# Local attention with 64-row transposes and four heads turned together, and the engine orders of that stage written anew

## The reference, cut to what matters

```python
# B, N, DIM = 8, 256, 128 here; DEPTH = 2, HEADS = 8, DIM_HEAD = 64, WINDOW = 64
h = shift_token(x)
q, k, v = split(h @ wqkv)                     # 8 heads of 64
q, k = l2norm(q) * qs, l2norm(k) * ksc
q, k = rotary_xpos(q, k)
# each window of 64 queries sees its own 64 keys and the 64 before
sim = einsum('bhwid,bhwjd->bhwij', bq * 8, bk)
mask = (i < j) | (i > j + WINDOW) | (j == -1)
attn = softmax(where(mask, -big, sim))
o = einsum('bhwij,bhwjd->bhwid', attn, bv)
x = x + o @ wo
h = layernorm(shift_token(x)) * lg + lb
a, g = split(h @ w1 + b1)
x = x + (a * gelu(g)) @ w2 + b2
```

## Time and profile before

| | |
|---|---|
| median of 3 runs | 911.72 us (910.61 to 911.75) |
| the profiled execution, its own time | 911.55 us |
| its span, first to last instruction | 909.8 us (so 1.7 us lie around it) |
| instructions | 22,535 |
| PE / PEld busy | 766.4 (84%) / 560.2 us (62%) |
| DVE busy | 662.8 us (73%) |
| ACT busy | 589.8 us (65%) |
| POOL busy | 527.3 us (58%) |
| mean granted TensorE clock | 0.930 of full speed |
| local attention stage (first to last `scores1`) | from 499.6 to 878 us |
| in it, one step | 23.9 us |

### The profile page before, as it was taken

The page is one execution under the profiler, slowest core; times in us unless marked ns, Lnnn a source line. Parts: engine busy times, 40 slices in busy tenths (PEclk is TensorE's granted clock), DMA queues, the critical chain, the costliest instruction groups (busy, mean ns, idle before and its releaser), DMA issues. The chain is left out here.

```text
span 909.8 us, 22535 instructions
## 1 busy us (share of the span) xinstructions
PE 766.4 (84%) x7262; PEld 560.2 (62%) x7262; DVE 662.8 (73%) x1986; ACT 589.8 (65%) x1784; POOL 527.3 (58%) x603
## 2 busy tenths in 40 slices
PE   5999999999987629946655789999999999998884
PEld 3666766666677528835532456666666666665564
DVE  5788888888858665535754677887888888877555
ACT  3688888888811107733433678888888888877660
POOL 4644545555435853348717677777777777776411
PEclk9999999999999759975877899999999999999998
DMA  8455444444300753421100000000000000000001
GB/s 216 159 181 180 161 173 169 168 175 163 127 2 16 236 165 91 115 65 44 32 1 0 1 1 2 2 2 1 1 2 1 2 2 1 2 1 2 13 2 35
DMA packets 61855, 61.71 MB, mean 68 GB/s; under 512 B 13243, under 2 KB 50606, under 8 KB 61614
## 3 DMA queue, kind: packets, MB, share of 16 engines
q1 hardware_dynamic: 59694, 56.10, 18.7%
q0 software_dynamic: 2048, 4.20, 1.5%
HBM read 17.55 MB, written 23.00 MB: 45 GB/s over the span
## 5 line engine op out<-in xcount | busy, mean ns | idle before, releaser
L641 POOL TENSOR_TENSOR scratch<-scratch 128x256 f32<-128x256 f32 (+1 forms) x128 | 105.7, 826 | 110.7 <-DVE scratch L1627 110.7
L1018 ACT ACTIVATE scratch<-psum,scratch 128x128 f32<-128x128 f32 x256 | 113.8, 458 | 49.4 <-DVE scratch L1974 47.6
L769 POOL TENSOR_TENSOR big<-big 128x512 f32<-128x512 f32 x64 | 81.2, 1269 | 70.6 <-DVE big L1955 70.6
L873 ACT ACTIVATE scratch<-psum,scratch 128x256 f32<-128x256 f32 x256 | 117.5, 479 | 3.6 <-DVE scratch L1645 3.6
L778 POOL TENSOR_TENSOR scratch<-scratch,mhalf 128x16 f32<-128x16 f32 x32 | 92.9, 2905 | 16.5 <-DVE scratch L1961 16.5
L1946 DVE TENSOR_REDUCE scratch<-big 128x8 f32<-128x512 f32 x64 | 43.7, 683 | 46.6 <-ACT big L992 46.6
L1125 PE MATMUL psum<-scratch 128*64 128x256 f32 x480 | 62.1, 379 | 1.6 <-DMA scratch<-xT 1.6
L1638 DVE TENSOR_TENSOR psum<-psum,causal 128x512 f32<-128x512 f32 x64 | 44.8, 699 | 20.4 <-PE psum L1149 20.1
L1149 PE MATMUL psum<-scratch 64*128 64x128 f32 (+1 forms) x512 | 59.2, 350 | 0.0
L1175 PE MATMUL psum<-scratch 128*64 128x256 f32 (+1 forms) x512 | 55.7, 338 | 2.2 <-DVE scratch L1633 2.2
L992 ACT ACTIVATE big<-psum 128x512 f32<-128x512 f32 x64 | 38.5, 602 | 29.0 <-PE psum L1398 28.1
(11 more groups left out here) (288 smaller groups left out, 2212.3 us busy)
## 6 DMA issues: line engine op xcount, KB each, us to landing
routed_in<-zfill SPq DMA_DIRECT2D x64, 256.0 KB, 2.3
scratch<-w_qkv SPq DMA_DIRECT2D x60, 193.0 KB, 2.2
scratch<-xT SPq DMA_DIRECT2D x60, 128.0 KB, 2.1
scratch<-routed_in SPq DMA_DIRECT2D x47, 64.0 KB, 1.8
routed_out<-scratch SPq DMA_DIRECT2D x23, 128.0 KB, 1.9
big<-in_L_ffn_W SPq DMA_DIRECT2D x1, 2048.0 KB, 8.7
stream<-in_L_attn_resid_pre SPq DMA_DIRECT2D x4, 256.0 KB, 3.9
big<-in_L_ffn_b SPq DMA_DIRECT2D x1, 1024.0 KB, 12.2
```

The lines of the kernel that those rows point to most:

```text
L641: pool.tensor_tensor(y, y, rs[s][:, t, :].unsqueeze(2).to_broadcast([P, 2, n]), ALU.mult).then_inc(b_p, 1)
L769: pool.tensor_tensor(qk[s][t][:, j * INNER:(j + 1) * INNER], t1[i % 2], t2[i % 2], ALU.add).then_inc(f_add, 1)
L873: last = act.activation(pr[s][:, t, h, :], scores_of(s)[:, h, t * S:(t + 1) * S], ACT.Exp, bias=nb[s][:, 2 * t + h:2 * t + h + 1], accum_o ...
L1018: last = act.activation(p1[k][:, h, t, :], bank(h)[:, t * P:(t + 1) * P], ACT.Exp, bias=nb1[k][:, h, t:t + 1], scale=rq8[s][:, t, 2 * a + ...
```

## The change

Four things are done together.

1. **q/k transposes.** `turn_qk` now has two pieces a unit (`half_` = 0, 1), each of which turns q and k of two pairs (four heads) with 16 transposes of 64 rows: rows 0 to 63 into bank 5, rows 64 to 127 into bank 3. ACT copies each bank out (`turned_out`, two copies of 512 columns a piece). It now waits for the rotated q too, and for DVE to have emptied bank 3.
2. **Probability transposes.** `turn_probs1` also has two pieces, each turning two pairs with 16 transposes of 64 rows into banks 2 and 3. It waits for both pairs' normalisation. ACT copies bank 2 (`probs_out`), DVE bank 3; `values1` does two pairs (12 products) at once into bank 2 and waits for both copies; `z_out` copies two pairs at once. `p1` has four buffers in place of two, `pt1` one that holds two pairs.
3. **The mask.** `scores1` writes the mask with four 64-row, 64-column products for a pair in place of two 128-row ones; the second array half needs the mask with its two row halves exchanged, `band_swapped`, which two DMAs from `band` fill near the start.
4. **The orders** of PE, ACT and DVE in a step are written anew; POOL's is the same.

```diff
             sp_.wait_ge(const_ready, 2)
+            load(band_swapped[0:WIN], band[WIN:P])
+            load(band_swapped[WIN:P], band[0:WIN])
...
             def expo(m, s, a):
                 act.wait_ge(f_nb, m * 4 + a + 1)
-                if later(m * 4 + a - 1):
-                    act.wait_ge(f_t, m * 4 + a - 1)
+                if later(m * 2 + a // 2 - 1):
+                    act.wait_ge(f_t, m * 2 + a // 2 - 1)
...
-            def probs_out(m, a):
-                act.wait_ge(f_t, m * 4 + a + 1)
-                act.activation(pt1[0].rearrange("p h t n -> p (h t n)"), bank(2), ACT.Copy).then_inc(f_pt0, 1)
+            def probs_out(m, half_):
+                act.wait_ge(f_t, m * 2 + half_ + 1)
+                act.activation(turned_probs_half(0), turned_probs(0), ACT.Copy).then_inc(f_pt0, 1)
...
+            def turn_qk(m, s, half_):
+                if half_ == 0:
+                    pe.wait_ge(f_kn, m + 1)
+                    pe.wait_ge(f_add, m * 4 + 4)
+                    pe.wait_ge(f_v, m * 2 + 2)
+                elif live(m + 2):
+                    pe.wait_ge(f_hT, m + 3)
+                if later(m * 2 + half_ - 1):
+                    pe.wait_ge(f_pt1, m * 2 + half_ - 1)
+                for j in range(2):
+                    for b_ in range(2):
+                        for t in range(TB):
+                            for r in range(2):
+                                rows = slice(r * DH, (r + 1) * DH)
+                                o = (j * PAIRS1 + 2 * half_ + b_) * P
+                                c = (j * 2 + b_) * P + t * DH
+                                mm = pe.transpose(bank(QK_TURNED[r])[:, c:c + DH], qk[s][t][rows, o:o + P], ident[rows, rows])
...
-                for h in range(2):
-                    pe.matmul(bank(h)[:, 0:S], identb[:], band[:].rearrange("p t n -> p (t n)"), start=True, stop=False,
-                              skip_group_check=True)
+                for u in range(2):
+                    for h in range(2):
+                        rows = slice(h * DH, (h + 1) * DH)
+                        pe.matmul(bank(h)[u * WIN:(u + 1) * WIN, 0:S], identb[rows, rows],
+                                  (band if u == h else band_swapped)[rows].rearrange("p t n -> p (t n)"),
+                                  start=True, stop=False, skip_group_check=True)
...
+            def turn_probs1(m, half_):
+                pe.wait_ge(f_p, m * 2 + half_ + 1)
+                pe.wait_ge(f_pp, m * 2 + half_ + 1)
+                if later(m * 2 + half_):
+                    pe.wait_ge(f_zsb, m * 2 + half_)
+                if half_ == 0:
+                    pe.wait_ge(f_trs, m * 4 + 4)
+                elif live(m + 1):
+                    pe.wait_ge(f_trs, m * 4 + 6)
+                for a in range(2):
+                    for h in range(2):
+                        for t in range(TB):
+                            for r in range(2):
+                                rows = slice(r * DH, (r + 1) * DH)
+                                mm = pe.transpose(turned_probs(r)[:, (a * 2 + h) * TB + t, :],
+                                                  p1[2 * half_ + a][rows, h, t, :], ident[rows, rows])
...
+            def values1(m, s, half_):
+                pe.wait_ge(f_pt0, m * 2 + half_ + 1)
+                pe.wait_ge(f_pt1, m * 2 + half_ + 1)
...
+                for a in range(2):
+                    for v, t, o, n in ((v1[s][:, 0, :], 0, 0, P), (vmid[s], 1, 0, WIN), (v1[s][:, 1, :], 1, WIN, WIN)):
...
+            def turned_out(m, s, half_):
...
+                for u in range(2):
+                    act.activation(qkT1[s][:, :, 2 * half_:2 * half_ + 2, u * P:(u + 1) * P],
+                                   bank(QK_TURNED[u]).rearrange("p (j b n) -> p j b n", j=2, b=2), ACT.Copy).then_inc(f_trs, 1)
...
+        def turned_probs(r):
+            return bank(2 + r).rearrange("p (b n) -> p b n", n=DH)
+        def turned_probs_half(r):
+            return pt1.rearrange("p a h t n -> p (a h t) n")[:, :, r * DH:(r + 1) * DH]
+        QK_TURNED = (5, 3)
...
             def step(n, s):
+                if live(n - 1): z_out(n - 1, 1 - s, 1)
                 if live(n + 2): square(n + 2, 0)
-                if live(n - 1): z_out(n - 1, 1 - s, 3)
-                if live(n): turned_out(n, s, 3)
                 if live(n): expo(n, s, 1)
+                if live(n + 1): value_out(n + 1, 1 - s, 0)
+                if live(n + 1): value_out(n + 1, 1 - s, 1)
                 if live(n): probs_out(n, 0)
...
                 if live(n - 1): gelus(n - 1)
+                if live(n): probs_out(n, 1)
                 if live(n + 2): square(n + 2, 3)
                 if live(n + 1): expo(n + 1, 1 - s, 0)
-                if live(n + 1): turned_out(n + 1, 1 - s, 2)
-                if live(n): z_out(n, s, 2)
+                if live(n + 1): turned_out(n + 1, 1 - s, 1)
```

More of the change, by code:

```diff
@@ L74, in build_program @@
         band = sb("band", [P, TB, P], BF16)
+        band_swapped = sb("band_swapped", [P, TB, P], BF16)
         shift = sb("shift", [P, P])
@@ L364, in build_program @@
         hT = two(from_scratch, S)
-        p1 = two(from_scratch, 2, TB, P)
-        pt1 = two(from_scratch, 2, TB, P)
+        p1 = [from_scratch(2, TB, P) for _ in range(PAIRS1)]
+        pt1 = from_scratch(2, 2, TB, P)
         ssx = from_scratch(TB, 2 * H1, 2)
@@ L765, in add_rot @@
                 j, t = 1 - i // 2, i % 2
-                if later(m * 4 - 4):
-                    pool.wait_ge(f_tr, m * 4 - 4)
+                if later(m * 2 - 2):
+                    pool.wait_ge(f_tr, m * 2 - 2)
                 pool.wait_ge(f_rot, m * 4 + i + 1)
@@ L797, in values_there @@
                 pool.wait_ge(f_v, m * 2 + 2)
-                if later(m * 4 - 4):
-                    pool.wait_ge(f_z, m * 4 - 4)
+                if later(m * 2 - 2):
+                    pool.wait_ge(f_z, m * 2 - 2)
             def window_values(s):
@@ L1017, in expo @@
                     for h in range(2):
-                        last = act.activation(p1[k][:, h, t, :], bank(h)[:, t * P:(t + 1) * P], ACT.Exp,
+                        last = act.activation(p1[a][:, h, t, :], bank(h)[:, t * P:(t + 1) * P], ACT.Exp,
                                               bias=nb1[k][:, h, t:t + 1],
@@ L1459, in scores1 @@
                 mm.then_inc(f_s, 1)
-            def turn_probs1(m, a):
-                pe.wait_ge((f_p, f_pp)[a % 2], m * 2 + a // 2 + 1)
-                if later(m * 4 + a - 1):
-                    pe.wait_ge(f_zsb, m * 4 + a - 1)
-                for h in range(2):
-                    for t in range(TB):
-                        mm = pe.transpose(bank(2 + a % 2)[:, (h * TB + t) * P:(h * TB + t + 1) * P],
-                                          p1[a % 2][:, h, t, :], ident[:])
+            def turn_probs1(m, half_):
[14 more added lines that the diff above has]
+                                                  p1[2 * half_ + a][rows, h, t, :], ident[rows, rows])
@@ L2043, in step @@
                 if live(n + 1): neg_max(n + 1, 1 - s, 0)
-                if live(n): probs_out(n, 3)
+                if live(n): probs_out(n, 1)
                 if live(n + 2): rotate(n + 2, 3)
```

112 lines of the change are left out of this document (38 added, 74 removed).

## The result

The changed kernel takes **952.53 us** (median of 4 runs, 950.60 to 953.56), the kernel before beside it 911.66 us (4 runs, 910.61 to 911.75). The ratio is **1.0449, 95% interval 1.0428 to 1.0469**: 4.5% slower. The forecast was 928 us, with a range up to 946; it had the sign and the waits, and not the size: the time lies 6.5 us above the range. The profiled execution took 953.56 us, its span is 951.8 us, 42.0 us longer than before.

What follows compares the result with a forecast made beforehand. PE was taken to bound the kernel, 22.7 of 23.9 us a step. PE's work falls 2.5 us, but three waits make the step 25.2 us; 13 x 1.3 = 17 us on 911.55 gives 928 us, range 884 to 946.

Steps and rivals of the forecast that it cites:

- the other way round: Cross-check of the new step: 20.2 us of PE work plus 4.8 us of waits are 25.0 us.
- Items 1 to 5: One step followed from `hidden` half 0 to the next through PE and DVE, with three waits: 25.2 us.
- item 4: PE waits 1.9 us ahead of `project1(n+2, 2)` for `rotate(n+2, 1)`, which now stands behind `residual_out` on DVE.
- Item 1: From `hidden` half 0 over DVE's `gate`, `normalise1(n, 0)` and `neg_max(n, 1)`, its small product taken as 0.47 us: 5.01 us.
- half clock on top of the forecast: Rival: waits halve PE's clock from `project_v` on; 946 us if in every step, 937 if in half; chance 0.12.
- the first wait: PE waits 1.7 us ahead of `project_v` for DVE's `rotate(n+2, 0)` to free bank 4.
- the second wait: PE waits 1.9 us ahead of `project1(n+2, 2)` for DVE's `rotate(n+2, 1)` to free bank 4.
- 13 x 1.3: Full steps 0 to 13, the first still filling, each 1.3 us longer: 17 us added to the kernel.
- Before and after them I see no difference that I can sign: Outside the full steps 0 to 13, no time was added or taken off.
- the rotations were not done in time (faster): Rival judged: rotations done when PE needs them, PE stays the bound; 865 to 902 us, middle 884; chance 0.24.
- the gains and waits did not cancel: Rival judged: all three waits 0.4 us shorter each, a step of 24.0 us, 912 us in all; chance 0.10.
- the halves overlap: Rival judged claimed the opposite: half transposes don't overlap, 1.5 us per four groups, 958 us; chance 0.02.

Runs made afterwards that it cites:

- e6: The kernel before with only the mask of `scores1` changed to four quarter products, transposes and orders as before: 891.59 us, ratio 0.9788.
- e5: The changed kernel with 8 whole transposes of 128 rows in place of each 16 halves, same banks, copy sizes and orders: 968.75 us, ratio 1.0618.
- e1: The changed kernel with seven unused identity products on PE ahead of `project1(n+2, 2)`, where PE waits anyway: 940.97 us, ratio 1.0325.
- e4: e23 with DVE's `normalise1(n, 0)` moved behind `neg_max(n, 1)` and `rotate(n+2, 0)`: 931.69 us, ratio 1.0229.
- e3: The changed kernel with DVE's `residual_out` put back behind `rotate(n+2, 1)` and `query_scales`, as in the kernel before: 931.04 us, ratio 1.0209.
- e23: The changed kernel with both moves, `hidden(n-1, 0)` ahead of `values1(n, 1)` on PE and `residual_out` behind `rotate(n+2, 1)` on DVE: 915.21 us, ratio 1.0049.
- e2: The changed kernel with `hidden(n-1, 0)` on PE moved ahead of `values1(n, 1)` and `turn_qk(n+1, 1)`: 927.22 us, ratio 1.0157.

## Why the prediction was right and wrong

- **What bounds the kernel before** (PE, with one wait of 1.18 us): right, and the reader was told that the loop over `expo` is as long as PE's work. That this wait hung on 0.02 us between two instructions was not seen: e6 takes 0.7 us of PE's work out of a step and gains 1.72.
- **PE's own work.** 16 halves 0.64 us (0.72 foretold), mask with scores 0.67 (0.71), two pairs of values 635.57 - 634.52 = 1.05 (1.03): each within 0.1 us. The whole is not: the step at full clock less its waits is 25.69 - 4.64 = 21.05 us, not 20.2. The changed pieces give back the 2.5 us, but the others take 0.9 more from start to start, `project1` 4.05 in place of 3.63, and groups that a wait follows run out alone (`attn_out` 2.02 in place of 1.86). The forecast does not rest on it, only the count "the other way round". That the price of each product would eat the gain of the halves, as the rule in the Trainium skill's "TensorEngine Tiling (Array Packing)", "Instruction Overhead", read as a bound would have it, is not what the runs show: 0.64 us against 0.97 for the same eight in whole ones, and e5 is 16 us slower.
- **Items 1 to 5, the loop and its three waits**: right in every link, 1.23 to 1.80, 1.93 and 0.68 us against 1.7, 1.9 and 0.9 (item 4's own terms, 0.40 + 1.9 - 0.5, make 1.8). The loop by itself is 25.42 us (e1) against 25.2.
- **Item 1, the row that was read wrongly.** That the normalisation and `scale_keys` "do run side by side" does not come out of the earlier trace rows. The 2.49 us there are two products. The first takes 1.04 us and ends at 623.95; the second, in POOL's order of time before, by itself:

```profile
623.91 1.49 POOL L784 TENSOR_TENSOR big<-big,scratch 128x512 f32<-128x512 f32 x1
```

  The normalisation, from 623.72 for 0.78 us, ends 0.55 us after the first product, and the second takes 0.45 us more than the first: they took turns. Beside `add_rot` the normalisation ends by the same 0.55 us after it (rows of e4: 661.71 against 661.17). So the Trainium skill's rule, which was set aside there, holds for both, and the 25.42 us lie in the 25.2 to 25.7 that were worked out by it. In six of the steps 3 to 12 the normalisation comes first, takes 0.69 us and holds `add_rot` up (1.72 us in place of 1.27), and the small product takes 0.47; in the other four `add_rot` is first, the normalisation takes 1.10 to 1.61 (1.28 in the row of the chain) and the small product 0.16. The 0.47 of the sum was picked between two ends: that six steps show just that is luck.
- **The sum: the step that failed is that the half clock was left out of it, as the rival "half clock on top of the forecast".** The prediction named the mechanism and priced it at 937 us for half of the steps, gave it 0.12, and hung it on the first wait, since `project_v` had once run slowly near a wait of 2.17 us. The runs show it behind the second wait, the longer of the two (1.93 in every step), in seven steps of ten. It costs 0.75 us a step on average, and 11.6 us in all (e1). With waits of 1.0 us at that place (e3, e23) it does not come in steps 3 to 12. Behind the same 1.93 us in e2, where the first wait is 0.60, it comes in two of ten, so the second wait is not enough by itself. The half clock alone would have made some 940 us (928 + 11.6), inside the range; the terms below took the time out of it.
- **The sum, second: "13 x 1.3".** The 23.9 us were taken for all full steps, but steps 1 and 2 of the kernel before take 22.74 and 22.93 us, and steps 0 to 2 lose 7.7 us in place of some 3. In step 2 it is the loop (25.1). In step 1 (25.5) it is mostly the clock: its second wait is 2.39 us, and in e1, at full clock, the step takes 23.77. Of the changed kernel, in the windows view:

```profile
536.00:561.50 25.50, 21.40 (x244) 14.15 (x244) 16.85 (x45) 19.28 (x54) 18.50 (x16) 0.93 0.01 2
```

  Step 13, which has waits of its own in both kernels, loses 3.3, of which e1 gives back 1.9.
- **"Before and after them I see no difference that I can sign"**, a term put at nothing without a reason: wrong for the end, by 5.2 us. In the last unit the loop's first part is longer still. DVE of the changed kernel in order of time, then PE:

```profile
904.43 1.26 DVE L2033 SCALAR_TENSOR_TENSOR scratch<-psum,vec,scratch 128x256 f32<-128x256 f32 x3 [3.44 <-PE psum L1539]
...
908.28 0.69 DVE L2001 TENSOR_TENSOR scratch<-scratch 128x512 f32<-128x512 f32 x1
```

```profile
911.86 0.39 PE L1450 MATMUL psum<-band,identb 64*64 64x256 bf16 x1 [4.00 <-ACT scratch L1028]
```

  `gate` comes late behind the late `hidden`, the first layer norm of the end stands on DVE between it and the normalisation, and PE waits 4.00 us for the exponential, where the kernel before waited 2.04; the clock is 0.50 after it. In e23, with the earlier `hidden`, the stretch from `scores1(15, 1)` to the end is 912.2 - 867.88 = 44.3 us in place of 47.5. Whether the 3.2 us ahead of unit 0 belong to the change stays open: the eight traces of the same program up to there have unit 0 at 505.24 (e1) to 508.50 us, most of them near 507.5, against 505.34 before.
- **The rivals that did not come**: the rotations were not done in time (faster), the gains and waits did not cancel, and the halves overlap as they did in the first block.

Open stays why three steps of ten keep the full clock behind a wait of the same 1.93 us, and eight of ten in e2. Taking the half transposes into the old order, pair by pair, was not tried: the halves write two banks at once, and there each bank is still being read for another pair.

## What to carry to other kernels

Follow the closed loop through all engines before counting what an engine saves: here 1.7 us of PE's work a step (22.7 to 21.05) were bought with three waits, of which two came from single lines in the orders, and 37 of the 41 us came back when those two lines were moved. Take a change apart and try its parts in the old order: the smallest part, the quarter mask, was alone worth 2.1%, and the whole change buried it. When a new wait on PE is nearly 2 us, put the lower clock after it into the sum, at the longest wait of the loop and not only where it was once seen; how often it comes is for a run to say.

## What was not expected of the hardware

- A wait of 1.93 us repeated in each step brought 3.4 us at half clock (granted 0.51) in seven of ten steps, and in two of ten where another wait of the step was shorter (e2). Useless products in that wait made the kernel 11.6 us faster.
- Two DVE products took turns with POOL's: the small one took 0.16 us alone and 0.18 to 1.26 behind one, and ended 0.02 us after it; the normalisation took 0.69 alone and up to 1.80 behind one, and ended some 0.55 us after it. A POOL product that came second was held up in its turn, `add_rot` to 1.72 us from 1.27, `scale_keys` to 1.49 from 1.04. Beside POOL's `inverse_norm`, which stands for 2.90 us in its row, both took what they take alone (0.16 and 0.69 us). Which comes first is set by the phase of the loop, to some hundredths of a microsecond, so a small gain on PE (e6) can be doubled by it, and a harmless move on DVE (e4) can cost 16 us.
- Four mask products on quarters of the array take 0.11 to 0.13 us together until the scores start, where two whole ones took 0.31.
